# Near keys per 64 queries, two heads side by side in the partitions, and one near score bank at a time

## The chip, the cores and the metric

The kernel runs on one NeuronCore of a Trainium2 chip. The metric is the device time of one execution in microseconds. Nothing is shared with other cores; the input is the same in every run.

## The reference, cut to what matters

A layernorm over `x` (4 x 2048 x 256, f32) feeds two branches that are added to `x`: a linear layer on values rounded to fp8, and an attention with 16 heads of width 16. In the attention, query `i` sees key `j` only if `j` is a multiple of 4 ("far" keys, 512 of them, the same for every query) or if it is close ("near" keys):

```python
allowed = (j % STRIDE == 0) | (jnp.abs(i - j) <= LOCAL)      # STRIDE 4, LOCAL 8
scores = jnp.where(allowed, scores, -jnp.inf)
attn = jax.nn.softmax(scores, axis=-1)
out = jnp.einsum('bhqk,bhkd->bhqd', attn, v)
```

The softmax subtracts the true maximum of each row, so the scores are made twice: once to find each query's maximum and once, with the maximum already subtracted, for the exponential.

## The kernel before

**Two stages.** `part_project` makes q, k, v and the linear branch, 512 rows at a time, and writes q, k and v to DRAM tables. `part_attend` then walks 64 steps: 4 batches x 4 groups of 4 heads (16 iterations) x 4 chunks of 512 queries. Every step's instructions are written out for each engine, so the order of work on TensorE (PE) is the order of calls in `tensor_attend`'s `body`.

**The heads of a group** are numbered h = 2p + f: f picks the half of the array's rows in which q and k of the head lie (partitions 0-50 or 64-114; `half(f)`), p is the pair. q and k are each three fp16 parts (48 rows), and 3 more rows carry the negated maximum.

**What a step does on each engine:**

- PE, maxima: 8 calls `far_unit(tile, p)` (L1105): queries of one 128-row tile against 512 far keys for both f, into two PSUM banks (`ps_u`, two such pairs of banks). 2 calls `near_unit(tiles)` (L1110 to L1127): for each of two query tiles, a mask matmul (L1116, 216 columns) and then 2 x 2 matmuls of 108 columns (L1123): the near window of 128 queries has 108 keys that are no multiples of 4.
- DVE: one `tensor_reduce` for each unit (L1012 far, 1024 elements; L1015 near, 864 elements), then `maximum()` (L995); POOL splits the result in bf16 parts (`negmax`), PE transposes it (`maxima`, L1061), ACT copies it (L946), and SP moves it into the q operand of the next step (L859). The maxima run ahead of the scores: the first AHEAD units of a step's list belong to the next step, the others to the one after.
- PE, scores: 8 calls `far(r, p)` (L1070): 128 far keys x 512 queries for both f, one PSUM bank each. 2 calls `near(p)` (L1072 to L1086): for each of 4 query tiles, two mask matmuls (L1080) and two score matmuls (L1083), 128 columns each, for both f at once, into two banks of 108 partitions.
- The banks of the scores are a ring of three (`S_BANKS`, `ps_s`): before it writes a bank, PE waits in `free_score` until ACT has read what was in it three entries before. A step has 21 entries: 16 far, 4 near, 1 for the maxima.
- ACT: one `Exp` for each score bank (L953 far, L958 near), 512 columns each, one copy of the result (L937, `copy_out`, after the bank of far (1,3)), one small copy of the maxima.
- PE, weighing (f32): `weigh(r)`: for each of 4 far rounds, 4 heads in 4 column strips of the array, 512 columns (L1142); for the near keys, 4 tiles x 4 heads, 128 columns (L1149). An f32 matmul appears as two instructions. All go into bank `ps_o`: one group of three rounds belongs to the step before, two to the step itself.
- SP issues all DMAs in one order: q and k of steps ahead (L90, L92, L100), v of the iteration ahead (`load_v`, one DMA for the far and three for the near keys, in four pieces over two steps), the sums (L851), shares and results.

**PE's order in a step of before** (W is a `weigh`, `u` a far unit, `nu` a near unit):

```
u(2,1) far(0,0) | W2 | far(0,1) u(1,0) u(0,0) far(2,1) | W3 | far(1,0) nu(0) u(2,0) far(1,1) | W4 near keys |
near(0) u(3,1) u(1,1) far(2,0) | W0 | maxima far(3,1) u(3,0) nu(1) far(3,0) | W1 | near(1) u(0,1)
```

Of the kernel before, what the change touches and what calls it, by code (L numbers as in the profile page):

```python
# [45 lines left out]
HALF = P // 2  # L46
# [4 lines left out]
MASK_K = WPAD + S - NS + WPAD  # L51
# [7 lines left out]
VR = D + 1  # L59
EPS = 1e-5  # L60
BANDS = ((1, 18), (6, 6), (21, 5))
# [17 lines left out]
def half(f, n=KR):  # L79

    return slice(f * HALF, f * HALF + n)
# [21 lines left out]
def part_project(nc, io, dram, keep, ctx):  # L103

    with ExitStack() as memory:
# [31 lines left out]
        v_sb = sb("v_sb", [P, 2, TT, NH, VR])  # L137
# [72 lines left out]
        def sync_project(sp):  # L210
# [13 lines left out]
            sp.dma_start(keep["mask_k"][:], io["near_k"].bitcast(BF16)).then_inc(keep["bands_loaded"], 16)  # L224
            sp.dma_start(keep["mask_q"][:], io["near_q"].bitcast(BF16)).then_inc(keep["bands_loaded"], 16)
# [53 lines left out]
        def gpsimd_project(pool):  # L279
# [5 lines left out]
            nc.gpsimd.memset(v_sb[:, 0, :, :, D:VR], 1.0).then_inc(v_set, 1)  # L285
            nc.gpsimd.memset(v_sb[:, 1, :, :, D:VR], 1.0).then_inc(v_set, 1)
# [23 lines left out]
        def scalar_project(act):  # L310
# [6 lines left out]
            def body(j, n):  # L317
# [27 lines left out]
                if main:  # L345
# [7 lines left out]
                    if not (isinstance(c, int) and c < 2):  # L353
                        act.wait_ge(v_stored[k], 16 * earlier(j, n))
                    nc.scalar.activation(
                        v_sb[:, k].rearrange("p t h w -> p (t h) w")[:, :, 0:D],
                        ps_v.rearrange("p a (t w) -> p (a t) w", w=D), ACT.Copy).then_inc(v_copied, 1)
# [267 lines left out]
UNITS = TT * PAIRS + TT // 2  # L625
# [3 lines left out]
AHEAD = 5  # L629
# [5 lines left out]
    ("near", 0), ("far", 2, 0), ("negmax",), ("far", 3, 1), ("far", 3, 0),  # L635
    ("near", 1),
# [3 lines left out]
    ("far", 2, 1), ("far", 1, 0), ("far", 0, 0), ("near", 0), ("far", 2, 0),  # L640
    ("far", 3, 1), ("far", 1, 1), ("far", 3, 0), ("near", 1), ("far", 0, 1),
# [17 lines left out]
def part_attend(nc, io, dram, keep, out, ctx, done):  # L659
# [69 lines left out]
    k_op, mask_k, mask_q = keep["k_op"], keep["mask_k"], keep["mask_q"]  # L729
    v_op = [keep["v_op"], sb("v_op1", [P, NS // P + S // P, HG * VR])]  # L730
    probs = sb("probs", [P, ROUNDS, HG, CH])
# [53 lines left out]
    def window(p, tile):  # L785
        return p * S + WSTEP * tile
# [3 lines left out]

    def close(tile):
        return WSTEP * tile
# [39 lines left out]
    def sync_attend(sp):  # L832
        def load_v(it, par, windows=range(-1, STRIDE - 1)):

            v = dram["v"][it // G, :, it % G * HG * VR:(it % G + 1) * HG * VR]
            for r in windows:
                if r < 0:
                    to, src = v_op[par][:, 0:NS // P, :], v[LOCAL:LOCAL + S, :].rearrange(
                        "(c p r) w -> r p c w", p=P, r=STRIDE)[0]
                else:  # L840
                    to = v_op[par][r:WIN:STRIDE - 1, NS // P:, :]
                    src = bass.AP(tensor=v.tensor, offset=v.offset + (1 + r) * NH * VR,
                                  ap=[[STRIDE * NH * VR, WIN // 3], [P * NH * VR, S // P], [1, HG * VR]])
                sp.dma_start(to, src).then_inc(v_loaded[par], 16)
# [69 lines left out]
        for k in range(2):  # L914
            sp.wait_ge(done["qk_stored"][k], 16 * 12 * B * CPB // 2)
            sp.wait_ge(done["v_stored"][k], 16 * B * CPB // 2)
        load_v(0, 0)
# [11 lines left out]
    def scalar_attend(act):  # L929
# [9 lines left out]
        def body(st):  # L939
            todo = st.entries()  # L940
            for kind in todo:
# [12 lines left out]
                else:  # L954
                    h = kind[1]
# [23 lines left out]
    def vector_attend(dve):  # L979

        def body(st):
# [16 lines left out]
            for i, kind in enumerate(MAXIMA):  # L998
# [14 lines left out]
                else:  # L1013
                    tile = 2 * kind[1]
                    ins = nc.vector.tensor_reduce(peak_near[:, :, tile:tile + 2].rearrange("q f t p -> q f (t p)"),  # L1015
                                                  banks[:, :, 0:2 * PAIRS * WIN].rearrange("q f (g w) -> q f g w",
# [344 lines left out]
```

## Time and profile before

| what | value |
| --- | --- |
| median of 3 runs | 1126.22 us (1123.71 to 1129.16) |
| span of the profiled execution | 1127.2 us; no time of its own is listed for that execution |
| busy: PE, DVE, ACT, POOL | 95%, 84%, 72%, 22% |
| attention steps | from about 247 us to about 1055 us of the span |
| projection, final projection | before and behind them |

A page of the profile lists busy time by engine, the span in 40 slices, the chain that ended last, and groups of instructions (line, engine, operation, output and inputs with shapes, count; then busy time and mean duration, and the idle time before them with what ended it). PEld is the weight load of a matmul, a separate instruction. The busy time of PE counts a matmul from its start to its modelled end, so back-to-back short matmuls overlap in it.

### The profile page before, as it was taken

The numbers are of one execution on the slowest core, as the hardware profiler recorded it, in microseconds if no ns is written. First come the engines' busy times: TensorE is split into PE (matmuls) and PEld (weight loads), VectorE is DVE, ScalarE is ACT, GpSimd is POOL, SyncE is SP. The second block draws the span as 40 slices with busy tenths as digits, with TensorE's granted clock in tenths as the row PEclk, the third lists the DMA queues.
The fourth block names the chain that finished last, engine by engine and source line by source line (L and its number), as shares of the span: only waits on it lengthen the run. The fifth ranks groups of instructions, "written<-read, shape, count | busy, mean of one in ns | idle before, by whom it ended". The sixth has DMA issues, their size and how long they took to land.

```text
span 1127.2 us, 28640 instructions
## 1 busy us (share of the span) xinstructions
PE 1070.1 (95%) x10945; PEld 484.3 (43%) x10945; DVE 948.4 (84%) x1203; ACT 811.9 (72%) x1524; POOL 248.4 (22%) x381
## 2 busy tenths in 40 slices
PE   5899999969999999999999999999999999999898
PEld 3566666623333333333333333333333333333387
DVE  5888877588999999999999999999898999999133
ACT  2444344327988898888888888888898888888700
POOL 1433333301121212212121212212121212222100
PEclk9999999968999999999999999999999999999999
DMA  6566666641232333333332333333333333231167
GB/s 188 184 197 206 206 209 209 196 111 44 81 87 81 99 91 85 87 103 104 95 107 82 112 91 105 89 96 111 94 99 93 99 94 94 86 84 48 55 216 246
DMA packets 167066, 134.21 MB, mean 119 GB/s; under 512 B 70652, under 2 KB 146172, under 8 KB 166924
## 3 DMA queue, kind: packets, MB, share of 16 engines
q1 hardware_dynamic: 164344, 128.19, 38.4%
q10 hardware_dynamic: 2592, 4.26, 1.1%
q8 instruction: 85, 1.39, 0.5%
q14 instruction: 45, 0.37, 0.1%
HBM read 71.26 MB, written 59.84 MB: 116 GB/s over the span
## 4 chain that ended last, share of the span: by engine, by line
PE 74%; DVE 12%; issue 7%; DMA 5%; ACT 2%; SPq 0%; DVEq 0%; ACTq 0%
PE ps_attend L1142 15%; PE ps_attend L1070 11%; DVE peak_far L1012 10%; PE ps_attend L1105 9%; PE ps_attend L1149 5%; PE ps_attend L1222 5%; PE ps_project L607 5%; PE ps_project L597 5%; PE ps_project L576 4%; PE ps_attend L1080 4%; DMA sums<-out_rows 3%; PE ps_attend L1116 3%; PE ps_project L540 2%; PE ps_attend L1083 2%; PE ps_attend L1123 2%
## 5 line engine op out<-in xcount | busy, mean ns | idle before, releaser
L1012 DVE TENSOR_REDUCE peak_far<-ps_attend 128x2 f32<-128x1024 f32 x512 | 608.7, 1221 | 42.7 <-PE ps_attend L1105 31.3
L953 ACT ACTIVATE probs<-ps_attend 128x512 f32<-128x512 f32 x1024 | 541.4, 598 | 49.4 <-PE ps_attend L1070 46.2
L1142 PE MATMUL ps_attend<-probs,v_op 128*17 128x512 f32 x2048 | 270.2, 600 | 0.0
L1070 PE MATMUL ps_attend<-q_op,k_op 51*128 51x512 f16 x1024 | 254.2, 387 | 4.9 <-ACT probs L953 3.3
L1105 PE MATMUL ps_attend<-k_op,q_op 48*128 48x512 f16 x1024 | 187.9, 388 | 25.7 <-DVE peak_far L1012 15.3
L958 ACT ACTIVATE probs<-ps_attend 108x512 f32<-108x512 f32 x256 | 138.9, 594 | 35.7 <-PE ps_attend L1083 35.7
L1070 PEld LDWEIGHTS ps_attend<-q_op,k_op 51*128 51x128 f16 x1024 | 76.8, 93 | 195.6 <-ACT probs L953 137.4
L819 POOL CAST negmax<-peak 128x16 bf16<-128x16 f32 x64 | 12.7, 198 | 612.8 <-DVE peak L995 612.8
L1015 DVE TENSOR_REDUCE peak_near<-ps_attend 128x8 f32<-128x864 f32 x128 | 131.0, 1023 | 10.5 <-PE ps_attend L1123 10.4
L810 POOL TENSOR_TENSOR out_rows<-out_rows,share_rows 128x512 f32<-128x512 f32 x64 | 81.4, 1272 | 65.4 <-DMA share_rows<-shares_dram 63.0
L1105 PEld LDWEIGHTS ps_attend<-k_op,q_op 48*128 48x128 f16 x1024 | 49.7, 94 | 98.6 <-DVE peak_far L1012 71.6
L1080 PEld LDWEIGHTS ps_attend<-mask_q,mask_k 48*108 48x108 bf16 x1024 | 60.0, 125 | 69.4 <-ACT probs L953 56.1
L1080 PE MATMUL ps_attend<-mask_q,mask_k 48*108 48x128 bf16 x1024 | 78.7, 228 | 0.8 <-ACT probs L953 0.8
L1083 PE MATMUL ps_attend<-q_op,k_op 51*108 51x128 f16 x1024 | 73.6, 218 | 0.0
L1149 PE MATMUL ps_attend<-probs,v_op 108*17 108x128 f32 x2048 | 68.3, 274 | 0.0
L328 ACT ACTIVATE qk_parts<-ps_project,ranges 128x1024 f16<-128x1024 f32 x16 | 17.8, 1114 | 68.6 <-PE ps_project L576 62.0
L297 POOL TENSOR_TENSOR quant<-quant,power 128x1024 f32<-128x1024 f32 x16 | 37.7, 2357 | 116.9 <-DVE qk_parts L436 80.3
L1116 PE MATMUL ps_attend<-mask_k,mask_q 48*128 48x216 bf16 x512 | 59.0, 260 | 4.1 <-DVE peak_far L1012 1.6
L1083 PEld LDWEIGHTS ps_attend<-q_op,k_op 51*108 51x108 f16 x1024 | 61.5, 126 | 0.0
L576 PE MATMUL ps_project<-xnT,wq 128*128 128x512 f32 x128 | 60.2, 614 | 1.2 <-ACT xnT L335 1.2
L1142 PEld LDWEIGHTS ps_attend<-probs,v_op 128*17 128x17 f32 x2048 | 34.0, 95 | 59.3 <-issue 58.6
L1123 PE MATMUL ps_attend<-k_op,q_op 48*128 48x108 f16 x1024 | 58.4, 210 | 0.0
(82 smaller groups left out, 1037.9 us busy)
## 6 DMA issues: line engine op xcount, KB each, us to landing
share_rows<-shares_dram SPq DMA_DIRECT2D x64, 256.0 KB
attn_dram<-out_rows SPq DMA_DIRECT2D x64, 256.0 KB, 5.5
q_dram<-qk_parts SPq DMA_DIRECT2D x96, 128.0 KB
k_dram<-qk_parts SPq DMA_DIRECT2D x96, 128.0 KB
q_op<-q_dram SPq DMA_DIRECT2D x128, 96.0 KB, 2.4
k_op<-k_dram SPq DMA_DIRECT2D x64, 144.0 KB, 3.1
v_dram<-v_sb SPq DMA_DIRECT2D x16, 544.0 KB, 5.1
base<-in_x SPq DMA_DIRECT2D x16, 512.0 KB, 5.2
```

The costliest lines, as they stand in the source:

```text
L576: last = nc.tensor.matmul(ps_q[:, m], wq[:, i, m * P:(m + 1) * P], xnT[:, k, i], start=(i == 0), stop=(i == KC - 1))
L953: ins = nc.scalar.activation(probs[:, r, h], ps_s[st.bank(kind)], ACT.Exp, scale=undo)
L958: ins = nc.scalar.activation(probs[0:WIN, ROUNDS - 1, h], ps_s[st.bank(kind)][0:WIN], ACT.Exp, scale=undo)
L1012: ins = nc.vector.tensor_reduce(peak_far[:, :, p, tile], banks, AX_X, ALU.max)
L1015: ins = nc.vector.tensor_reduce(peak_near[:, :, tile:tile + 2].rearrange("q f t p -> q f (t p)"), banks[:, :, 0:2 * PAIRS * WIN].rearrange ...
L1070: nc.tensor.matmul(bank, k[half(f, KM), keys], q[half(f, KM), p], start=True, stop=True).then_inc(s_ready, 1)
L1080: nc.tensor.matmul(banks[f][0:WIN, cols], mask_k[half(f), at_mask:at_mask + WIN], mask_q[half(f), tile * P:(tile + 1) * P], start=True, st ...
L1083: ins = nc.tensor.matmul(banks[f][0:WIN, cols], k[half(f, KM), at:at + WIN], q[half(f, KM), p, cols], start=False, stop=True)
L1105: nc.tensor.matmul(banks[f], q[half(f), p, tile * P:(tile + 1) * P], k[half(f), strided(p):strided(p) + NS], start=True, stop=True).then_i ...
L1116: nc.tensor.matmul(banks[f][:, whole].rearrange("q (p w) -> q p w", p=PAIRS), mask_q[half(f), st.queries(d) * CH + tile * P:st.queries(d) ...
L1142: ins = nc.tensor.matmul(ps_o[h * VW:h * VW + VR], v[:, r, h * VR:(h + 1) * VR], probs[:, r, h], start=(r == 0), stop=False)
L1149: ins = nc.tensor.matmul(ps_o[h * VW:h * VW + VR, t * P:(t + 1) * P], v[0:WIN, tile, h * VR:(h + 1) * VR], probs[0:WIN, r, h, t * P:(t + 1 ...
```

## The change

**Window.** A window of near keys now belongs to 64 queries (`HALF`), not 128: 60 keys (`WIN`), 32 windows per row of 2048.

**Near scores.** `near()` fills two banks, one for each p. Bank p holds head f = 0 in partitions 0-59 and head f = 1 in 64-123. For each bank by itself: wait for it, one mask matmul of 512 columns (62 rows, 124 output partitions), then 8 tiles x 2 f score matmuls of 64 columns (51 rows, 60 outputs: half of the rows and half of the columns of the array), and one semaphore increment. A step has 19 ring entries instead of 21, and ACT makes 2 near exponentials of 124 x 512 instead of 4 of 108 x 512. `probs_near` has two buffers.

**Near maxima.** One near unit a step: two mask matmuls of 480 columns (one for each f) and 4 x 2 x 2 x 2 = 32 matmuls of 60 columns (48 rows, 64 outputs: the queries of half a tile). DVE reduces 960 elements once instead of 864 twice. `AHEAD` is 3 instead of 5.

**Weighing.** Near: 8 tiles x 2 pairs, 64 columns, 124 rows and 49 outputs: the v operand (`v_near`) holds zeros where the other head's keys are. v is laid out with the heads of the two pairs interleaved, so weights are read with a step of two; the far round 0 takes 32 outputs instead of 17.

**Loads.** v of an iteration comes in 7 DMAs instead of 4 (near rows of 34 elements for each f); POOL zeroes `v_near` at the start; one mask table instead of two.

**Order.** PE's order in a step becomes:

```
u(2,1) far(0,0) | W2 | u(1,0) far(0,1) u(0,0) far(2,1) | W3 | nu far(1,0) u(2,0) far(1,1) | W4 near keys |
u(3,1) maxima near u(1,1) far(2,0) | W0 | u(3,0) far(3,1) u(0,1) far(3,0) | W1
```

```diff
-WIN = (P + 2 * LOCAL) // STRIDE * (STRIDE - 1)
-WSTEP = P // STRIDE * (STRIDE - 1)
+WIN = (HALF + 2 * LOCAL) // STRIDE * (STRIDE - 1)
+WSTEP = HALF // STRIDE * (STRIDE - 1)
+NEAR = HALF + WIN
+MASK_ROWS = WIN + 2
+VP = 2 * VR
+VT = 2 * VW + VP
+VM = VW + VR
...
+            for par in range(2):
+                nc.gpsimd.memset(keep["v_near"][par][:], 0.0).then_inc(pads_set, 1)
...
-UNITS = TT * PAIRS + TT // 2
+UNITS = TT * PAIRS + 1
-AHEAD = 5
+AHEAD = 3
...
+                for f in range(2):
+                    to = v_near[par][f * HALF + r:f * HALF + WIN:STRIDE - 1, :, f * 2 * VW:f * 2 * VW + VP]
+                    src = bass.AP(tensor=v.tensor, offset=v.offset + (1 + r) * NH * VR + f * VP,
+                                  ap=[[STRIDE * NH * VR, WIN // 3], [HALF * NH * VR, NT], [1, VP]])
+                    sp.dma_start(to, src).then_inc(v_loaded[par], 16)
...
-                    if kind in OPENS and st.n >= 1:
-                        act.wait_ge(pv_done, ROUNDS * st.at())
-                    ins = nc.scalar.activation(probs[0:WIN, ROUNDS - 1, h], ps_s[st.bank(kind)][0:WIN], ACT.Exp,
-                                               scale=undo)
+                    if kind in OPENS and st.n >= 2:
+                        act.wait_ge(pv_done, ROUNDS * st.at(-1))
+                    ins = nc.scalar.activation(probs_near[0:NEAR, st.n % 2, kind[1]], ps_s[st.bank(kind)][0:NEAR],
+                                               ACT.Exp, scale=undo)
...
+        def score_near(st):
 
             q, k = q_op[:, st.slot()], k_op[st.parity()]
+            for p in range(PAIRS):
+                bank = free_score(st, ("near", p))
+                nc.tensor.matmul(bank[0:NEAR], masks[half(p, MASK_ROWS), MASK_KS],
+                                 masks[half(p, MASK_ROWS), shown(MASK_Q, HALF, st.queries())], start=True, stop=False)
+                for t in range(CH // HALF):
+                    cols, at = slice(t * HALF, (t + 1) * HALF), window(p, st.queries() * CH // HALF + t)
+                    for f in range(2):
+                        ins = nc.tensor.matmul(bank[half(f, WIN), cols], k[half(f, KM), at],
+                                               q[half(f, KM), p, cols], start=False, stop=(t == CH // HALF - 1))
+                ins.then_inc(s_ready, 1)
...
+            for f in range(2):
+                mask = masks[half(f, MASK_ROWS), shown(MASK_K, WIN, st.queries(d))]
+                nc.tensor.matmul(banks[f][:, 0:TT * PAIRS * WIN].rearrange("q (t p w) -> q t p w", t=TT, p=PAIRS),
...
+            for t in range(TT):
                 for p in range(PAIRS):
...
+                    for u in range(2):
+                        tile = 2 * t + u
+                        at = window(p, st.queries(d) * CH // HALF + tile)
+                        for f in range(2):
+                            ins = nc.tensor.matmul(
+                                banks[f][half(u, HALF), (t * PAIRS + p) * WIN:(t * PAIRS + p + 1) * WIN],
+                                q[half(f), p, tile * HALF:(tile + 1) * HALF], k[half(f), at],
...
+                n = VW if r == 0 else VR
                 for h in range(HG):
+                    ins = nc.tensor.matmul(ps_o[h * VW:h * VW + n], far[:, columns_of(r, h, n)], probs[:, r, h],
                                            start=(r == 0), stop=False)
             else:
                 pe.wait_ge(s_used, st.entry(LASTS["near",], d))
+                for t in range(CH // HALF):
+                    tile, cols = st.queries(d) * CH // HALF + t, slice(t * HALF, (t + 1) * HALF)
+                    for p in range(PAIRS):
+                        ins = nc.tensor.matmul(ps_o[half(p, VM), cols], near[0:NEAR, tile, p:p + 2 * VM - 1:2],
+                                               probs_near[0:NEAR, (st.n + d) % 2, p, cols],
+                                               start=False, stop=(t == CH // HALF - 1))
```

## Rows read from the trace of the kernel before

**Rows 1.** The page: busy time of PE, granted clock in 40 slices.

```profile
PE 1070.1 (95%) x10945; PEld 484.3 (43%) x10945; DVE 948.4 (84%) x1203; ACT 811.9 (72%) x1524; POOL 248.4 (22%) x381
...
PEclk9999999968999999999999999999999999999999
```

**Rows 2.** Groups from 400 to 1000 us, shapes apart: busy, mean ns, idle before.

```profile
L1012 DVE TENSOR_REDUCE peak_far<-ps_attend 128x2 f32<-128x1024 f32 x377 | 448.3, 1221 | 27.4 <-PE ps_attend L1105 18.6 <-issue 1.1
L953 ACT ACTIVATE probs<-ps_attend 128x512 f32<-128x512 f32 x754 | 398.7, 597 | 36.7 <-PE ps_attend L1070 34.4
L1142 PE MATMUL ps_attend<-probs,v_op 128*17 128x512 f32 x1504 | 197.9, 598 | 0.0
...
L958 ACT ACTIVATE probs<-ps_attend 108x512 f32<-108x512 f32 x188 | 102.0, 594 | 25.6 <-PE ps_attend L1083 25.6
L1015 DVE TENSOR_REDUCE peak_near<-ps_attend 128x8 f32<-128x864 f32 x94 | 96.0, 1022 | 7.9 <-PE ps_attend L1123 7.9
```

**Rows 3.** Timeline of PE, one step of 12.62 us: start, length, line, count.

```profile
602.38 0.23 PE L1061 MATMUL ps_attend<-ident_bf,negmax 128*128 128x128 bf16 x1
602.55 0.39 PE L1070 MATMUL ps_attend<-q_op,k_op 51*128 51x512 f16 x2
602.77 0.38 PE L1105 MATMUL ps_attend<-k_op,q_op 48*128 48x512 f16 x2
603.20 0.27 PE L1116 MATMUL ps_attend<-mask_k,mask_q 48*128 48x216 bf16 x2
603.30 0.26 PE L1123 MATMUL ps_attend<-k_op,q_op 48*128 48x108 f16 x4
603.39 0.26 PE L1116 MATMUL ps_attend<-mask_k,mask_q 48*128 48x216 bf16 x2
...
603.94 1.05 PE L1142 MATMUL ps_attend<-probs,v_op 128*17 128x512 f32 x8
604.92 0.26 PE L1080 MATMUL ps_attend<-mask_q,mask_k 48*108 48x128 bf16 x2
605.02 0.22 PE L1083 MATMUL ps_attend<-q_op,k_op 51*108 51x128 f16 x2
605.08 0.22 PE L1080 MATMUL ps_attend<-mask_q,mask_k 48*108 48x128 bf16 x2
...
606.59 1.05 PE L1142 MATMUL ps_attend<-probs,v_op 128*17 128x512 f32 x8
607.58 0.39 PE L1070 MATMUL ps_attend<-q_op,k_op 51*128 51x512 f16 x2
...
608.97 1.05 PE L1142 MATMUL ps_attend<-probs,v_op 128*17 128x512 f32 x8
609.96 0.39 PE L1070 MATMUL ps_attend<-q_op,k_op 51*128 51x512 f16 x2
...
611.35 1.07 PE L1149 MATMUL ps_attend<-probs,v_op 108*17 108x128 f32 x32
612.35 0.26 PE L1080 MATMUL ps_attend<-mask_q,mask_k 48*108 48x128 bf16 x2
...
612.86 0.64 PE L1105 MATMUL ps_attend<-k_op,q_op 48*128 48x512 f16 x4
...
614.02 1.05 PE L1142 MATMUL ps_attend<-probs,v_op 128*17 128x512 f32 x8
615.00 0.23 PE L1061 MATMUL ps_attend<-ident_bf,negmax 128*128 128x128 bf16 x1
```

**Rows 4.** Timeline of PE's weight loads in that step: in brackets the wait before.

```profile
611.03 0.09 PEld L1070 LDWEIGHTS ps_attend<-q_op,k_op 51*128 51x128 f16 x1 [0.18 <-ACT probs L953]
```

**Rows 5.** Timeline of ACT in that step.

```profile
610.38 2.08 ACT L953 ACTIVATE probs<-ps_attend 128x512 f32<-128x512 f32 x4 [0.29 <-PE ps_attend L1070]
...
613.05 1.08 ACT L958 ACTIVATE probs<-ps_attend 108x512 f32<-108x512 f32 x2
```

**Rows 6.** Timeline of the DMA issues on SP, the same step.

```profile
615.57 1.61 SPq L859 DMA_DIRECT2D q_op<-negmax_rows  x2
```

More of the change, by code:

```diff
@@ L634 @@
     ("far", 0, 0), ("far", 0, 1), ("far", 2, 1), ("far", 1, 0), ("far", 1, 1),
-    ("near", 0), ("far", 2, 0), ("negmax",), ("far", 3, 1), ("far", 3, 0),
-    ("near", 1),
+    ("negmax",), ("near", 0), ("far", 2, 0), ("far", 3, 1), ("far", 3, 0),
 )
@@ L639 @@
 MAXIMA = (
-    ("far", 2, 1), ("far", 1, 0), ("far", 0, 0), ("near", 0), ("far", 2, 0),
-    ("far", 3, 1), ("far", 1, 1), ("far", 3, 0), ("near", 1), ("far", 0, 1),
+    ("far", 2, 1), ("far", 1, 0), ("far", 0, 0), ("near",), ("far", 2, 0),
+    ("far", 3, 1), ("far", 1, 1), ("far", 3, 0), ("far", 0, 1),
 )
@@ L785, in window, with columns_of, shown @@
     def window(p, tile):
-        return p * S + WSTEP * tile
+        at = p * S + WSTEP * tile
+        return slice(at, at + WIN)
+    def columns_of(r, h, n):
+        first = (r * 2 + h % 2) * VP + h // 2
+        return slice(first, first + 2 * n - 1, 2)
+    def shown(columns, tile, queries):
+        first = columns.start + (0 if queries == 0 else 2 if queries == CPB - 1 else 1) * tile
+        return slice(first, first + columns.stop - columns.start - 2 * tile)
     def strided(p):
         return WPAD + p * S + S - NS
-    def close(tile):
-        return WSTEP * tile
     def gpsimd_attend(pool):
@@ L1129, in weigh @@
-        def weigh(st, d, r, tiles=range(TT)):
-            v = v_op[st.parity(d)]
+            for f in range(2):
+                mask = masks[half(f, MASK_ROWS), shown(MASK_K, WIN, st.queries(d))]
+                nc.tensor.matmul(banks[f][:, 0:TT * PAIRS * WIN].rearrange("q (t p w) -> q t p w", t=TT, p=PAIRS),
+                                 masks[half(f, MASK_ROWS), MASK_QS],
+                                 mask.rearrange("r (t w) -> r t w", t=TT).unsqueeze(2).broadcast_to(
+                                     [MASK_ROWS, TT, PAIRS, WIN]), start=True, stop=False)
@@ L1132, in weigh @@
+        def weigh(st, d, r):
+            far, near = v_far[st.parity(d)], v_near[st.parity(d)]
             if r == 0:
                 if st.queries(d) == 0:
-                    pe.wait_ge(v_loaded[st.parity(d)], 64 * (st.half_iteration(d) + 1))
+                    pe.wait_ge(v_loaded[st.parity(d)], 16 * 7 * (st.half_iteration(d) + 1))
                 if st.n + d >= 1:
@@ L1158, in far_unit, with near_unit @@
                 unit(st, ("far", tile, p))
-            def near_unit(tiles):
-                unit(st, ("near", tiles))
+            def near_unit():
+                unit(st, ("near",))
             def far(r, p):
@@ L1173, in maxima, with weigh_last @@
                     score_peaks(st)
-            def weigh_last(r, tiles=range(TT)):
+            def weigh_last(r):
                 if st.exists(-1):
-                    weigh(st, -1, r, tiles)
+                    weigh(st, -1, r)
             def weigh_own(r):
@@ L1195, in body @@
             weigh_last(4)
-            near(0)
             far_unit(3, 1)
+            maxima()
+            near()
             far_unit(1, 1)
```

145 lines of the change are left out of this document (54 added, 91 removed).

## The prediction

> **What bounds the kernel now.** I read the page first: PE is busy 95% of the span at full granted clock over nearly all slices [rows 1]. That number alone misleads, because a short matmul counts until its modelled end. So I then read the groups of the attention stage, and last the timeline of one step on each engine. The near reduction L1015 ran 94 times in 600 us, so 47 steps took 12.77 us each on average [rows 2]; most repeat one pattern of 12.62 us (602.38 to 615.00) [rows 3], and a few take some tenths longer. DVE has 8 far reductions at about 1.17 us apart and 2 near ones: it is busy for some 11.8 us of the 12.62. ACT's 21 reads of PSUM take less: four exponentials need 2.08 us [rows 5], about 0.5 each. Neither fills the step, and PE's own streams don't either.
>
> What sets the step is seen in PE's timeline when it is cut at the five weighs. A far weigh takes 0.98 us (606.59 to 607.58), the near one 1.00 (611.35 to 612.35) [rows 3]. Between them lie five gaps, each of which fills four score banks. With three banks in the ring, the fourth fill must wait for the exponential of the first. For the gap before W4: far(1,0) starts at 609.96, its exponential at 610.38 [rows 5], it lasts 0.60, the freed bank's weight load starts at 611.03 after a wait on ACT [rows 4], 512 columns at 2.4 GHz are 0.21, and the weigh starts at 611.35, which leaves 0.11 for emptying the array before its f32 column strips begin. So a gap that opens with a far pair costs 1.40 (607.58 to 608.97, 609.96 to 611.35, 602.55 to 603.94), one that opens with near(p) costs 1.67 (612.35 to 614.02, 604.92 to 606.59) [rows 3]. The sum is 3 x 1.40 + 2 x 1.67 + 0.16 for the maxima + 4 x 0.98 + 1.00 = 12.62. That is the measured step: **a chain of PE streams and one exponential's latency per gap**, in which units hide for nothing between the first and the fourth fill.
>
> **The change, gap by gap.** DVE saves about 2 x 1.02 - 1.13 = 0.9 us a step (864 elements take 1.02, 1024 take 1.22, so 960 take about 1.13) and ACT two exponentials, 1.0 us [rows 2, 5]. In this account both are worth nothing: the cover is the PE chain, and each keeps more than 1.5 us of slack. What counts is what PE does between the weighs.
>
> A pair of 512-column matmuls costs a slot of 0.22 (602.55 to 602.77) [rows 3]. In the new order one unit stands before the first far pair of three gaps, where no exponential hides it.
> - Before W3 and before W1: 0.22 + 1.40 = 1.62 each, 3.24 together.
> - Before W2, one unit and one far pair, the ring not full: 0.22 + 0.22 + 0.11 for emptying = 0.55.
> - Before W4: nu + 1.40.
> - Before W0: u(3,1) 0.22, emptying 0.11 because the maxima matmul uses the whole array, maxima 0.16, near bank 0 (N), near bank 1 (N), u(1,1) and far(2,0). The second bank of far(2,0) reuses near bank 0. From that bank's end to the weigh is 1.16 at least (near(0) of before ends at 612.86, W0 starts at 614.02 [rows 3]), or else N + 0.22 + 0.22 + 0.11, whichever is longer.
>
> *N.* The mask is 512 columns, 0.22. The 16 fills go in 8 pairs (f = 0 and 1 in opposite corners of the array). In before, two matmuls of different row halves start together (a group x2 is as long as one) and a pair takes 0.06 at 128 columns (605.02 to 605.08); a pair of 108 columns takes about 0.048 (x4 from 603.30 to 603.39) [rows 3]. At 64 columns a pair lies between 0.027 (the columns alone) and 0.059 (the nearest row); I take 0.035, nearer the columns, since both rows scale with them, so 0.28. Mask and fills use different shapes of the array. Where before changes shape it pays about 0.11: the maxima matmul holds PE 0.17 (602.38 to 602.55) for 128 columns, which are 0.05 [rows 3]. No row shows this particular change, from 64 x 128 to 64 x 64; bounds 0 and 0.11. I take 0.11, since every change of shape that rows show pays it, and twice per bank (in and out). N = 0.22 + 0.28 + 0.22 = 0.72.
>
> *nu.* The mask: 216 columns take 0.10 (603.20 to 603.30) [rows 3], 480 take 0.21. The 32 fills use all four corners; the far weigh shows four column strips at once (8 matmuls of 0.60 in 1.05) [rows 2, 3], so I take 8 groups of four at 0.035, 0.28 (bounds 0.22, and 32 x 0.030 = 0.96 if they go one by one at half the pair rate of before). Two changes of shape, 0.22. nu = 0.71, against 0.38 for each of two before (two halves of 0.19, 603.20 to 603.39) [rows 3].
>
> *Near weigh.* 32 matmuls of 64 columns, two strips at once, stream exactly as much as 32 of 128 columns, four at once. The weights are 49 columns instead of 17; hidden as long as a load is shorter than its stream. 1.00 to 1.44 (if two such loads go one after the other: 49 f32 columns in two passes are 0.041 each at 2.4 GHz, against a stream of 0.053 for both); I take 1.05. Round 0 with 32 outputs: nothing to 0.03, hidden in a stream of 0.43.
>
> The gap before W0 is 0.22 + 0.11 + 0.16 + 0.72 + max(1.16, 0.72 + 0.55) = 2.48. The step: 3.24 + 0.55 + (0.71 + 1.40) + 2.48 + 3.92 + 1.05 = **13.35 us against 12.62: +0.73, times 64 steps = +47 us**. Against the profiled execution (span 1127.2, no other time listed for it) that is 1174; the three runs have a median of 1126.2, 1 us below its span, so the forecast is **1173 us**.
>
> The rest is hidden, and its price if the cover goes is small: the POOL zeroing ends long before POOL's first sum; the first scores come one near reduction earlier, at most 1 us gained [rows 2]; three more v DMAs per iteration sit on SP ahead of the sums, shares and maxima. The maxima's DMA is the one to watch: it was issued from 615.57 to 617.18 [rows 6], 4.8 us after W4's end, and far(0,0) needs it. In the new order far(0,0) comes 2.37 + 0.98 + 1.62 + 0.98 + 0.22 = 6.2 us after W4's end; in before it was 1.67 + 0.98 + 0.16 + 1.40 + 0.98 + near(1) 0.51 (as 612.35 to 612.86) + two units 0.44, also about 6.2 [rows 3]. So nothing is taken. If it were late by a whole 1 us in half of the steps, that is 32 us. Behind the waiting far(0,0) all of PE would stand.
>
> A rule of the Trainium skill speaks against the change. TensorEngine Tiling, Key Properties, says that changing the tiling mode drains TensorE; in its terms, mask and fill are different modes. The rows agree for the changes that before makes (0.11 each); without any such cost at the fills the forecast would be the rival "no emptying" below.
>
> **The rivals.**
> 1. *No emptying between mask and fills*, everything else as forecast: N = 0.50, nu = 0.49, gap before W0 0.49 + 0.50 + 1.16 = 2.15, step 12.80; +0.18, +12 us: 1138 (1130 to 1146). For it: only the column half changes, and the row halves stay. Against: entering and leaving the maxima matmul costs.
> 2. *The small matmuls go one at a time.* Near fills alone: N = 0.22 + 16 x 0.030 + 0.22 = 0.92, gap 2.88, step +1.13, +72 us: 1199. The unit's as well: nu = 1.39, step +1.81, +116 us: 1242. For it: the fills of f = 0 and 1 now write one bank, where in before they wrote two; and there are twice as many small matmuls for the columns. Against: in before pairs start together. The Trainium skill bears on it: TensorEngine Tiling, Gotcha 1, says that different row tiles can't access the same PSUM bank simultaneously, which would give the first of these two times; TensorE: Matmul & The Clock Gate, Part 1, puts the least distance of two matmul starts at about 25 ns, which would give nearly the second. No row shows one bank written by both halves; against the second rule, rows show starts together in different tiles.
> 3. *Faster: masks and fills stream side by side.* A mask occupies one row half only; if the fills of the other half run beside it and no shape change costs anything, N = 0.43, nu = 0.42, the gap before W2 0.44, the gap before W0 0.38 + 0.43 + 1.16 = 1.97, the near weigh 0.95; step 3.24 + 0.44 + 1.82 + 1.97 + 3.92 + 0.95 = 12.34, -0.28, -18 us: 1108. It decides as soon as near stage, near unit and near weigh together fall under the 2.78 us that they take in before. For it: DVE and ACT are then lighter, so nothing else holds the step. Against: the 0.11 at every change of shape.
>
> **Chances and range.** Forecast 0.48 (own range 1148 to 1192), rival 1 0.13, rival 2 0.19, rival 3 0.16, late DMAs or something unseen 0.04. The range reaches down to rival 3's neighbourhood and up between the two forms of rival 2: 1112 to 1225. A measurement tells about 0.5%, 5.6 us, from no change: faster 0.16; within 0.5% a part of rivals 1 and 3, 0.10; slower 0.74.
>
> **What would show it.** Right: a step of about 13.3 us; three gaps of about 1.6 (one 2.1) where the fourth fill waits for ACT; PE starting the first fill 0.3 after its mask and the pairs of fills 0.03 to 0.04 apart; DVE and ACT with clearly more idle time ended by PE. Wrong: fills 0.015 or less apart per matmul with no pause behind the mask (rivals 1, 3), or 0.025 to 0.03 per matmul (rival 2); a weight load of far(0,0) that waits for a DMA; a near weigh well over 1.1 us. The weakest number is the pause at a change of shape: six of them a step, 42 us in all.

## The result

The changed kernel takes **1160.53 us** (median of 4 runs, 1159.62 to 1161.34) against 1126.45 (4 runs) before: ratio **1.0307**, 95% interval 1.0286 to 1.0328, so 34 us or 3.1% slower. The forecast was 1173, +47 us, by a step of 13.35 us instead of 12.62.

The page of the changed kernel: PE is busy as before, DVE and ACT have lost the work that the change takes from them (49 and 64 us of busy time, against [rows 1]), and the time went up.

```profile
PE 1082.1 (93%) x11713; PEld 468.0 (40%) x11713; DVE 899.3 (78%) x1139; ACT 747.5 (64%) x1396; POOL 253.8 (22%) x383
...
PEclk9999999959999999999999999999999999999999
```

The groups of the changed kernel from 400 to 1000 us (busy, mean ns, idle before it), which answer to [rows 2]: 46 near reductions in 600 us, so about 13.0 us a step by this count, and DVE and ACT idle far longer in front of far work, both ended by PE.

```profile
L1030 DVE TENSOR_REDUCE peak_far<-ps_attend 128x2 f32<-128x1024 f32 x362 | 435.7, 1215 | 78.9 <-PE ps_attend L1120 77.0
L972 ACT ACTIVATE probs<-ps_attend 128x512 f32<-128x512 f32 x724 | 378.5, 600 | 109.4 <-PE ps_attend L1087 109.4
...
L1032 DVE TENSOR_REDUCE peak_near<-ps_attend 128x16 f32<-128x960 f32 x46 | 53.3, 1158 | 20.2 <-PE ps_attend L1137 19.3 <-PE ps_attend L1120 0.8
```

PE's timeline over one step of the changed kernel (start, length, line, shapes, count), which answers to [rows 3]. L1165 is the near weigh, L1158 the far one, L1120 a far unit, L1087 far scores, L1094 and L1099 mask and fills of a near bank, L1127 and L1137 those of the near unit.

```profile
602.65 1.10 PE L1165 MATMUL ps_attend<-probs_near,v_near 124*49 124x64 f32 x32
603.69 0.39 PE L1120 MATMUL ps_attend<-k_op,q_op 48*128 48x512 f16 x2
604.01 0.23 PE L1078 MATMUL ps_attend<-ident_bf,negmax 128*128 128x128 bf16 x1
604.17 0.42 PE L1094 MATMUL ps_attend<-masks 62*124 62x512 bf16 x1
604.52 0.42 PE L1099 MATMUL ps_attend<-q_op,k_op 51*60 51x64 f16 x16
604.88 0.42 PE L1094 MATMUL ps_attend<-masks 62*124 62x512 bf16 x1
605.24 0.42 PE L1099 MATMUL ps_attend<-q_op,k_op 51*60 51x64 f16 x16
...
606.13 1.07 PE L1158 MATMUL ps_attend<-probs,v_far 128*32 128x512 f32 x8
607.13 0.39 PE L1120 MATMUL ps_attend<-k_op,q_op 48*128 48x512 f16 x2
...
608.42 0.39 PE L1087 MATMUL ps_attend<-q_op,k_op 51*128 51x512 f16 x1 [0.25 <-ACT probs L972]
608.74 1.05 PE L1158 MATMUL ps_attend<-probs,v_far 128*17 128x512 f32 x8
609.73 0.39 PE L1120 MATMUL ps_attend<-k_op,q_op 48*128 48x512 f16 x2
...
610.26 1.05 PE L1158 MATMUL ps_attend<-probs,v_far 128*17 128x512 f32 x8
611.25 0.39 PE L1120 MATMUL ps_attend<-k_op,q_op 48*128 48x512 f16 x2
...
612.86 1.05 PE L1158 MATMUL ps_attend<-probs,v_far 128*17 128x512 f32 x8
613.85 0.38 PE L1127 MATMUL ps_attend<-masks 62*128 62x480 bf16 x2
614.15 0.44 PE L1137 MATMUL ps_attend<-k_op,q_op 48*64 48x60 f16 x32
614.53 0.39 PE L1087 MATMUL ps_attend<-q_op,k_op 51*128 51x512 f16 x2
...
615.92 1.11 PE L1165 MATMUL ps_attend<-probs_near,v_near 124*49 124x64 f32 x32
```

Cut at the weighs, it reads term by term against the prediction:

| term | forecast | measured | from |
| --- | --- | --- | --- |
| near weigh | 1.05 | 1.04 | 602.65 to 603.69 |
| gap before W0 | 2.48 | 2.44 | 603.69 to 606.13 |
| a near bank, N | 0.72 | 0.71 | 604.17 to 604.88 |
| gaps before W1 and W3 | 1.62 each | 1.61 each | 607.13 to 608.74, 611.25 to 612.86 |
| gap before W2 | 0.55 | 0.53 | 609.73 to 610.26 |
| near unit | 0.71 | 0.68 | 613.85 to 614.53 |
| gap before W4 | 2.11 | 2.07 | 613.85 to 615.92 |
| four far weighs | 3.92 | 3.97 | 1.00 + 3 x 0.99 |
| step | 13.35 | 13.27 | 602.65 to 615.92 |

Every term lies within 0.05 us. A fourth fill still waits for ACT in the gaps before W1, W3 and W4 (the wait of 0.25 at 608.42 is one of them). Yet 64 x 0.65 is 42 us, and 34 were measured. Between the fourth and the last copy of the maxima (L946, L965) lie 60 steps: 764.1 us in before, 12.735 each, and 795.9 in the changed kernel, 13.264 each. Nearly all steps of the changed kernel are alike; before had some that took up to 13.8. The difference of these sums is 31.8 us, that of the two spans 32.3. The spans also tell of which executions the traces are: each run of the changed kernel takes 1.8 us more than its span (1161.34 against 1159.5), so the profiled execution of before, of 1127.2, would take about 1129.0 (an estimate), 2.6 above the median. Its irregular steps are then probably more than those of a median execution.

DVE waits for the DMA of the sums in some of these steps (engine, line, waited for: total, times, longest, 400 to 1000 us of before); the changed kernel's waits have no such row.

```profile
DVE shares L988 <- DMA sums<-out_rows: 7.4, 8, 1.4
```

### The profile page after: what moved, and what is told of

Same layout as the page of the kernel before. It is cut to its first block, busy times and chain, and to the rows that moved or that the text cites. A ratio compares the mean times of both kernels' runs of the same rounds, so it can differ in the third digit from the quotient of the medians.

```text
span 1159.5 us, 29841 instructions
## 1 busy us (share of the span) xinstructions
PE 1082.1 (93%) x11713; PEld 468.0 (40%) x11713; DVE 899.3 (78%) x1139; ACT 747.5 (64%) x1396; POOL 253.8 (22%) x383
## 4 chain that ended last, share of the span: by engine, by line
PE 84%; ACT 10%; DVE 2%; DMA 2%; issue 1%; SPq 0%; DVEq 0%; ACTq 0%
PE ps_attend L1158 22%; PE ps_attend L1087 14%; ACT probs L972 10%; PE ps_attend L1120 9%; PE ps_attend L1165 6%; PE ps_attend L1234 4%; PE ps_project L615 4%; PE ps_project L605 4%; PE ps_project L584 4%; PE ps_attend L1094 4%; PE ps_attend L1099 4%; PE ps_project L548 2%; PE ps_attend L1137 2%; PE ps_attend L1127 2%; PE ps_project L594 1%
## 5 line engine op out<-in xcount | busy, mean ns | idle before, releaser
L1087 PE MATMUL ps_attend<-q_op,k_op 51*128 51x512 f16 x1024 | 271.5, 384 | 49.0 <-ACT probs L972 48.8
L1158 PE MATMUL ps_attend<-probs,v_far 128*17 128x512 f32 (+1 forms) x2048 | 272.2, 604 | 0.0
L1120 PE MATMUL ps_attend<-k_op,q_op 48*128 48x512 f16 x1024 | 201.6, 389 | 8.1 <-DVE peak_far L1030 6.1
L1087 PEld LDWEIGHTS ps_attend<-q_op,k_op 51*128 51x128 f16 x1024 | 69.7, 95 | 171.3 <-ACT probs L972 149.5
L1120 PEld LDWEIGHTS ps_attend<-k_op,q_op 48*128 48x128 f16 x1024 | 49.4, 93 | 201.0 <-issue 103.4
L976 ACT ACTIVATE probs_near<-ps_attend 124x512 f32<-124x512 f32 x128 | 76.4, 597 | 35.5 <-PE ps_attend L1099 28.2
L1032 DVE TENSOR_REDUCE peak_near<-ps_attend 128x16 f32<-128x960 f32 x64 | 74.1, 1158 | 28.7 <-PE ps_attend L1137 27.7
L1165 PE MATMUL ps_attend<-probs_near,v_near 124*49 124x64 f32 x2048 | 70.7, 222 | 0.0
L1158 PEld LDWEIGHTS ps_attend<-probs,v_far 128*17 128x17 f32 (+1 forms) x2048 | 36.2, 100 | 81.2 <-issue 56.6
L1165 PEld LDWEIGHTS ps_attend<-probs_near,v_near 124*49 124x49 f32 x2048 | 61.3, 125 | 15.1 <-issue 15.1
L615 PE MATMUL ps_project<-wv,xnT 128*128 128x256 f32 x256 | 57.9, 379 | 0.0
L605 PE MATMUL ps_project<-xnT,wk 128*128 128x512 f32 x128 | 57.6, 593 | 0.0
L1094 PE MATMUL ps_attend<-masks 62*124 62x512 bf16 x128 | 54.9, 429 | 0.0
L1099 PE MATMUL ps_attend<-q_op,k_op 51*60 51x64 f16 x2048 | 54.8, 194 | 0.0
L615 PEld LDWEIGHTS ps_project<-wv,xnT 128*128 128x128 f32 x256 | 48.6, 190 | 13.4 <-issue 7.7
```

The source lines that it names most:

```text
L605: last = nc.tensor.matmul(ps_k[:, m], wk[:, i, m * P:(m + 1) * P], xnT[:, k, i], start=(i == 0), stop=(i == KC - 1))
L615: last = nc.tensor.matmul(ps_v[:, t // 2, t % 2 * H:(t % 2 + 1) * H], xnT[:, k, i, t * P:(t + 1) * P], wv[:, i], start=(i == 0), stop=(i = ...
L1087: nc.tensor.matmul(bank, k[half(f, KM), keys], q[half(f, KM), p], start=True, stop=True).then_inc(s_ready, 1)
L1094: nc.tensor.matmul(bank[0:NEAR], masks[half(p, MASK_ROWS), MASK_KS], masks[half(p, MASK_ROWS), shown(MASK_Q, HALF, st.queries())], start=T ...
L1099: ins = nc.tensor.matmul(bank[half(f, WIN), cols], k[half(f, KM), at], q[half(f, KM), p, cols], start=False, stop=(t == CH // HALF - 1))
L1120: nc.tensor.matmul(banks[f], q[half(f), p, tile * P:(tile + 1) * P], k[half(f), strided(p):strided(p) + NS], start=True, stop=True).then_i ...
```

## The experiments

Each ran in turn with the kernel before on one chip, so the ratios to before are the numbers to compare; times in parentheses are ratio x 1126.45. For the changed kernel the ratio is 1.0307.

### Masks in the shape of the fills

```diff
-                nc.tensor.matmul(bank[0:NEAR], masks[half(p, MASK_ROWS), MASK_KS],
-                                 masks[half(p, MASK_ROWS), shown(MASK_Q, HALF, st.queries())], start=True, stop=False)
+                for f in range(2):
+                    n, at = (HALF, WIN)[f], MASK_KS.start + f * HALF
+                    nc.tensor.matmul(bank[half(f, n)], masks[half(f, MASK_ROWS), at:at + n],
+                                     masks[half(f, MASK_ROWS), shown(MASK_Q, HALF, st.queries())],
+                                     start=True, stop=False)
```

> The changed kernel with each near bank's mask made by two matmuls on the two opposite corners of the array that the fills use (64 rows x 64 columns each, 512 columns, both side by side) instead of one matmul on 64 x 128. Shape-change theory: the two pauses inside each bank go, so a bank takes about 0.22 + 0.25 instead of 0.71 us, the gap before W0 falls from 2.44 to about 2.1 (near bank 0's end plus 1.16 becomes its floor), the step by 0.3, the time by about 20 us from 1160.5 to 1140. Rival, the extra time of a near bank is the price of many small matmuls: there are now two more of them, so no gain, 1160 to 1162.

Ratio 1.0151, 1.0131 to 1.0170 (1143.5): 17 us gained. PE's timeline of this kernel, from the near weigh's end to W0:

```profile
607.27 0.39 PE L1123 MATMUL ps_attend<-k_op,q_op 48*128 48x512 f16 x2
607.60 0.23 PE L1078 MATMUL ps_attend<-ident_bf,negmax 128*128 128x128 bf16 x1
607.75 0.40 PE L1096 MATMUL ps_attend<-masks 62*64 62x512 bf16 x2
608.00 0.40 PE L1102 MATMUL ps_attend<-q_op,k_op 51*60 51x64 f16 x16
608.24 0.38 PE L1096 MATMUL ps_attend<-masks 62*64 62x512 bf16 x2
608.46 0.40 PE L1102 MATMUL ps_attend<-q_op,k_op 51*60 51x64 f16 x16
...
609.41 1.07 PE L1161 MATMUL ps_attend<-probs,v_far 128*32 128x512 f32 x8
```

The same 16 fills take 0.24 (608.00 to 608.24) where they took 0.36, and a mask 0.22 to 0.25 where it took 0.35; the bank is 0.49 instead of 0.71 although it has one matmul more. The gap is 2.14, and near bank 0's end to W0 is 1.17, the floor that the prediction had put at 1.16; both banks together are 0.38 shorter (1.04 from 607.75 to 608.79, against 1.42), and this floor keeps 0.08 of it. So the pause of about 0.12 between 64 x 128 and 64 x 64 is real. The mask is still bf16, and the f16 fills still add to it, so neither of these makes the pause. The small matmuls cost little more than their columns, 0.030 for a pair.

### Both near banks masked, then both filled

```diff
-            for p in range(PAIRS):
-                bank = free_score(st, ("near", p))
+            banks = [free_score(st, ("near", p)) for p in range(PAIRS)]
+            for p, bank in enumerate(banks):
                 nc.tensor.matmul(bank[0:NEAR], masks[half(p, MASK_ROWS), MASK_KS],
                                  masks[half(p, MASK_ROWS), shown(MASK_Q, HALF, st.queries())], start=True, stop=False)
+            for p, bank in enumerate(banks):
                 for t in range(CH // HALF):
```

> The changed kernel with both near banks claimed and masked first and then both filled, instead of bank by bank. Shape-change theory: two of the four changes of shape at the near banks go; the gap before W0 falls by 0.2 us, the time by about 12 us to 1148. Rival, claiming both banks at once waits for ACT longer than it saves: no gain or a loss of up to 10 us. Rival, pauses don't depend on shape: no change.

Ratio 1.0221, 1.0199 to 1.0243 (1151.3): 9 to 10 us gained over the changed kernel. Its typical step is 13.10 instead of 13.27, 64 x 0.17 = 11 us. Claiming the second bank early cost nothing. The number was met, but not for the reason expected:

```profile
612.66 0.39 PE L1121 MATMUL ps_attend<-k_op,q_op 48*128 48x512 f16 x2
...
613.14 0.43 PE L1094 MATMUL ps_attend<-masks 62*124 62x512 bf16 x2
613.50 0.67 PE L1100 MATMUL ps_attend<-q_op,k_op 51*60 51x64 f16 x32
...
614.94 1.07 PE L1159 MATMUL ps_attend<-probs,v_far 128*32 128x512 f32 x8
```

Two of the four changes of shape are gone, and the two masks, which lie in different row halves, now run side by side: 0.36 for both, where one had taken 0.35. The two near banks take 0.96 (613.14 to 614.10) instead of 1.42. Of these 0.46 only 0.16 reach the step. Near bank 0 is filled no sooner: its last fill starts 1.08 behind the near weigh (613.74), against 1.07 in the changed kernel. The last fill of far(2,0) waits for this bank, its weight load stands 0.41 us for ACT, and W0 comes 1.20 after that last near fill, as in the run above. In the changed kernel it came 1.37 after. So the gain is the way down to the floor, not two pauses of 0.11.

### Three units put back under the exponential

```diff
-            far_unit(1, 0)
             far(0, 1)
+            far_unit(1, 0)
...
-            near_unit()
             far(1, 0)
+            near_unit()
...
-            far_unit(3, 0)
             far(3, 1)
+            far_unit(3, 0)
```

> The changed kernel with three neighbours swapped in PE's order: far(0,1) before u(1,0), far(1,0) before the near unit, far(3,1) before u(3,0), so that each gap opens with a far pair and the unit lies under the exponential's latency. Chain theory: two gaps fall from 1.61 to 1.40, one from 2.07 to about 1.45; the step by 1.0 us, the time by 55 to 67 us to about 1100, below the kernel before. Rival, PE's streams are the bound and their order does not matter: no change, 1160. Rival, DVE then gets its units in clumps and becomes the bound: a gain of less than 30 us.

Ratio 0.9837, 0.9817 to 0.9856 (1108.1): 52 us faster than the changed kernel and 18 us faster than before. PE's timeline, the gaps before W4 and W1:

```profile
602.67 0.39 PE L1087 MATMUL ps_attend<-q_op,k_op 51*128 51x512 f16 x2
...
604.10 1.10 PE L1165 MATMUL ps_attend<-probs_near,v_near 124*49 124x64 f32 x32
...
608.58 0.39 PE L1087 MATMUL ps_attend<-q_op,k_op 51*128 51x512 f16 x2
...
609.97 1.05 PE L1158 MATMUL ps_attend<-probs,v_far 128*17 128x512 f32 x8
```

The gaps are 1.43 (expected 1.45) and 1.39 (1.40); the step of 12.20 is 1.07 shorter. 64 x 1.07 would be 68 us. Most of the missing 16 is in irregular steps: the mean of the 60 is 12.424, which makes 60 x 0.22 = 13 us. far(0,0) stood for the DMA of the maxima, up to 2.1 us at a time (columns as above, 400 to 1000 us). PEld and PE are two instruction streams of one engine that stand in the same steps, so the two rows below must not be added.

```profile
PEld ps_attend L1087 <- DMA q_op<-negmax_rows: 13.6, 14, 2.1
...
PE ps_attend L1087 <- DMA q_op<-negmax_rows: 9.4, 9, 1.8
```

### The same three swaps in the kernel before, the other way round

```diff
-            far(0, 1)
             far_unit(1, 0)
+            far(0, 1)
...
-            far(1, 0)
             near_unit(0)
+            far(1, 0)
...
-            far(3, 1)
             far_unit(3, 0)
+            far(3, 1)
```

> The kernel before with nothing but three neighbours of PE's order swapped the way the change has them: u(1,0) ahead of far(0,1), the near unit ahead of far(1,0), u(3,0) ahead of far(3,1). Chain theory: two gaps grow by 0.22 us, one by 0.38, the step from 12.62 to 13.4; with before's scattered DMA waits then covered the time rises by 44 to 52 us to 1170 to 1178, more than the whole change costs. Rival, the change's cost comes from its small matmuls and masks and the order is neutral: no change from before.

Ratio 1.0404, 1.0386 to 1.0421 (1172.0): the order alone costs the kernel before 46 us, more than the whole change costs it. Its typical step is 13.43, as expected (13.4). In PE's timeline the gap before W4 is 1.77 (603.15 to 604.92), where it was 1.40 [rows 3]; the gap before W3 is 1.60 (613.99 to 615.59), and the one before W1 is 1.77 with the maxima's 0.16 in it (608.57 to 610.34):

```profile
603.15 0.27 PE L1116 MATMUL ps_attend<-mask_k,mask_q 48*128 48x216 bf16 x2
...
604.92 1.07 PE L1149 MATMUL ps_attend<-probs,v_op 108*17 108x128 f32 x32
```

### More work for DVE, more work for ACT

The first edit makes the near reduction twice, once into a spare tile that nothing reads:

```diff
+                    nc.vector.tensor_reduce(keep['peak_spare'][:].rearrange("q f t p -> q f (t p)"),
+                                                  banks[:, :, 0:TT * PAIRS * WIN].rearrange("q f (g w) -> q f g w",
+                                                                                            w=WIN), AX_X, ALU.max)
```

> The changed kernel with the near reduction on DVE made a second time into a spare tile, 1.1 us more DVE work per step (69 us in all), more than the change had saved there. Chain theory: DVE has over 2 us of slack per step, so 0 to +6 us. Rival, DVE's work counts in the step: up to +69 us.

Ratio 1.0373, 1.0343 to 1.0402 (1168.5): 7 to 8 us for 69 us of work. The typical step went from 13.27 to 13.35: in the trace u(3,1) starts 1.11 us after the near weigh instead of 1.04 (606.57 to 607.68), since its pair of banks is released later. The expectation of at most 6 us was slightly passed.

```profile
606.57 1.11 PE L1168 MATMUL ps_attend<-probs_near,v_near 124*49 124x64 f32 x32
607.68 0.39 PE L1123 MATMUL ps_attend<-k_op,q_op 48*128 48x512 f16 x2
```

The second adds two exponentials to a step:

```diff
                 ins.then_inc(s_used, 1)
+                if kind in (("far", 2, 3), ("far", 3, 1)):
+                    nc.scalar.activation(keep["spare"][:], keep["wo"][:].rearrange("p k f -> p (k f)"), ACT.Exp)
```

> The changed kernel with two extra exponentials of 128 x 512 on ACT in each step (from SBUF into a spare tile, behind far (2,3) and far (3,1), where ACT stood idle for 1.0 and 0.5 us): 1.1 us more ACT work a step, 70 us in all, about what the change saved there. Chain theory: they lie in idle time and no exponential of a gap starts later, 0 to +5 us. Rival, ACT's work counts in the step: up to +70 us.

Ratio 1.0293, 1.0276 to 1.0310 (1159.5), the interval overlaps that of the changed kernel: nothing for some 70 us of ACT work. ACT's timeline has the extra exponential (L980) in what was idle time:

```profile
606.22 2.07 ACT L972 ACTIVATE probs<-ps_attend 128x512 f32<-128x512 f32 x4 [0.45 <-PE ps_attend L1090]
608.15 0.65 ACT L980 ACTIVATE spare<-wo 128x512 bf16<-128x512 f32 x1
```

So giving ACT back as much as the change took from it, 1.0 us a step, costs nothing where it is idle, and giving DVE back a little more than the 0.9 that it had lost costs 7 to 8 us: so the lighter DVE bought no more than about that. That an exponential in another place of ACT's order would be free as well is not shown.

### Do two halves of the rows write one bank at a time?

```diff
-                for t in range(CH // HALF):
-                    cols, at = slice(t * HALF, (t + 1) * HALF), window(p, st.queries() * CH // HALF + t)
-                    for f in range(2):
+                for f in range(2):
+                    for t in range(CH // HALF):
+                        cols, at = slice(t * HALF, (t + 1) * HALF), window(p, st.queries() * CH // HALF + t)
```

> The changed kernel with the near fills of a bank in another order: all eight tiles of head f = 0, then all eight of f = 1, so that neighbours lie in the same corner of the array and can't run side by side. If fills of opposite corners do overlap in one bank (about 0.03 us per pair in the changed kernel's trace), a bank takes 0.25 us longer, the gap before W0 0.5, the time 30 us more: 1190. Rival, matmuls of two row halves can't write one bank at the same time, so they already go one by one: no change, 1160.

Ratio 1.0473, 1.0450 to 1.0495 (1179.7): 19 us more than the changed kernel, not 30 and not 0. A bank's fills take 0.50 (611.95 to 612.45) instead of 0.36:

```profile
611.95 0.57 PE L1099 MATMUL ps_attend<-q_op,k_op 51*60 51x64 f16 x16
612.45 0.42 PE L1094 MATMUL ps_attend<-masks 62*124 62x512 bf16 x1
```

The rival is refuted: fills of opposite corners do run side by side in one bank. The size was mis-expected, since this order doesn't keep them apart. Read in slices of 0.01 us, the trace has four fills start one after the other up to 612.07, eight more from 612.10 to 612.22, about two every 0.03 us, and then the last four one by one, 0.03 us apart. It doesn't say which fill is which, but this fits f = 1 setting in while f = 0 still has about four to go.

### The scattered waits of before

```diff
-TURN = 8
+TURN = 9
```

> The kernel before with the reciprocal of the sums one reduction later in DVE's order (in front of the last unit of a step instead of the last but one). In before, 8 of 47 steps had DVE wait for the sums' DMA, 7.4 us in 600, and the mean step was 12.77 instead of 12.62; in the changed kernel that wait is gone. If this wait is what makes before's steps irregular, and so what the change gave back beside its longer steps: a gain of 5 to 9 us on before, ratio 0.992 to 0.996. Rival, the irregular steps come from something else: ratio 1.000 or above.

Ratio 0.9983, 0.9970 to 0.9996: 2 us, not 5 to 9. DVE's wait for the sums is gone from this kernel's waits, but far(0,0) now waits for the maxima's DMA, which it never did in before (300 to 1000 us, columns as above):

```profile
PEld ps_attend L1070 <- DMA q_op<-negmax_rows: 6.7, 26, 0.9
```

Its mean step is 12.647 instead of 12.735 in its one profile, 5.3 us in 60 steps, of which the two spans keep 3.3 (1127.2 and 1123.9). That before's profile is of an execution slower than its median is part of the rest. So the wait for the sums is part of before's irregular steps, and behind it stands the next DMA, almost as late. Four steps of 12.90 to 12.92, one in 16, are in both traces; their cause is open. The changed kernel has the reciprocal of the sums in front of its last unit too, for its `TURN` is 8 of nine units. But a longer step alone takes most of the wait away: in the run above with before's units first, a step of 13.43, DVE waited 2.1 us for the sums from 300 to 1000 us, against 7.4 in before.

### The maxima's DMA ahead of the second piece, and all together

Both kernels below have this edit on SP, and the three swaps:

```diff
                 move_sums(st)
-            load_piece(st, 1)
             if ("negmax",) in st.entries():
                 move_negmax(st)
+            load_piece(st, 1)
```

> The swapped order of the earlier run (three units hidden) with one more edit: SP issues the DMA of the maxima ahead of the second piece of k or v instead of behind it. In that run's trace far(0,0) waited 23 us of 600 for this DMA, in steps whose v pieces stood ahead of it. DMA theory: these waits go, worth 15 to 30 us: 1080 to 1095 against 1108. Rival, the wait moves to k, v or the sums: less than 5 us gained.

Ratio 0.9731, 0.9713 to 0.9749 (1096.1): 12 us under the run with the swaps alone; expected were 15 to 30. The mean step is 12.207 (it was 12.424), its typical one 12.20, so the waits are gone and there was no more to gain from them. The expectation was too high because its 23 us are the two rows above added, 13.6 and 9.4, which are largely the same waits seen twice.

Where the DMA had been late is seen in SP's queue in the run with the swaps alone. The two near DMAs of v ahead of the maxima's two transfers take 1.7 us to issue. But in nine steps the issue of the two itself took 2.3 to 3.7 us instead of 1.5 to 1.6, and these nine are those behind the nine fetches of finished heads (L782, two DMAs of 256 KB):

```profile
622.31 1.34 SPq L782 DMA_DIRECT2D heads<-attn_dram  x2
...
631.00 1.67 SPq L862 DMA_DIRECT2D v_near<-v_dram  x2
632.72 2.94 SPq L877 DMA_DIRECT2D q_op<-negmax_rows  x2
...
644.46 1.66 SPq L862 DMA_DIRECT2D v_near<-v_dram  x2
646.16 1.54 SPq L877 DMA_DIRECT2D q_op<-negmax_rows  x2
```

In the 21 other steps with the same two v DMAs ahead it took 1.54 to 1.55, once 1.87, so these v DMAs alone don't stretch it. With the maxima's DMA ahead of them it takes 1.52 to 1.61 in every step. How the fetch comes to act a step later is open.

The last one adds the corner masks of the first experiment, the same for the near unit (four mask matmuls of 64 outputs), and the maxima matmul right behind W4:

```diff
-            far_unit(3, 1)
             maxima()
+            far_unit(3, 1)
```

> Everything that the account says is loss taken out of the changed kernel: masks on the corners for near banks and near unit, three units hidden, the maxima matmul right behind W4, the maxima's DMA ahead of the second piece. Account: gaps 1.39 + 1.39 + 1.39 + 0.53 + 2.04, weighs 5.01, step 11.75 us; times 64 that is 29 us under the swapped order's 12.20, so about 1060 to 1070 if the maxima's DMA is in time. Rival, DVE (10.9 us of work a step, two pairs of banks) becomes the bound: 12.0 to 12.2 us a step, 1080 to 1095.

Ratio **0.9566**, 0.9548 to 0.9585 (1077.6): 4.3% faster than before, 83 us faster than the changed kernel, but 8 us over the expected range. PE's timeline of its step, 11.89 us long:

```profile
603.78 0.23 PE L1078 MATMUL ps_attend<-ident_bf,negmax 128*128 128x128 bf16 x1
603.94 0.39 PE L1123 MATMUL ps_attend<-k_op,q_op 48*128 48x512 f16 x2
604.26 0.40 PE L1096 MATMUL ps_attend<-masks 62*64 62x512 bf16 x2
...
605.91 1.07 PE L1163 MATMUL ps_attend<-probs,v_far 128*32 128x512 f32 x8
```

The gap before W0 is 2.13, as with the corner masks alone: with the maxima first, the pause moved from before them to behind the unit (603.94 to 604.26 is 0.32 for a slot of 0.22). The near unit gained nothing either: its pause between mask and fills became one between the far pair ahead of it and the mask. The account had counted both as gains, 0.14 us a step, 9 us. The mean step is 11.989, 0.1 over the typical one; the trace shows waits for the sums and for the maxima's DMA again. The rival, DVE as the bound, lay at 12.0 to 12.2 us a step; the typical step of 11.89 still has PE's gaps of 1.39 and 1.44, and PE stood for DVE only 2.5 us in 600, so DVE is not the bound yet. But it idles only about 1.1 us of such a step (0.61, 0.22 and 0.23), so little room is left below it.

## Why the prediction was right, and where it was off

**The bound.** Right. PE's chain with one exponential's latency per gap gave 12.62 for before and every gap of the changed kernel within 0.05 us. The swaps in both directions (52 us gained, 46 lost) and 70 us of extra work on ACT for nothing show it. "DVE and ACT worth nothing" holds for ACT; for DVE it holds but for 7 to 8 us, the price of its near reduction made twice.

**Units in front of the first far pair.** Right: 1.61, 1.61 and the near unit in full. This is what made the kernel slower. With these swaps undone, the same change is faster than before. The prediction summed this loss but did not single it out; it called the pauses the weakest number. Those are the smaller part: taking three of the four at the near banks away gave 17 us.

**The pause at a change of shape.** Taken as 0.11 from other shapes, bounds 0 and 0.11; the corner masks show 0.10 to 0.13 per change. The two changes of one near bank cost 0.22 of its 0.71 us. The rule of the Trainium skill (TensorEngine Tiling, Key Properties: changing the tiling mode drains TensorE) agrees with these runs.

**The small matmuls.** Taken as 0.035 per pair, measured 0.030; with the pause a little over 0.11 the two small errors nearly cancel in N (0.71 for 0.72), which is luck. The unit's 32 fills take 0.38 with the pause behind them, so four at a time, as taken. Rival 2 is refuted, also in the form of the Trainium skill's TensorEngine Tiling, Gotcha 1: with outputs in different partitions of one bank the two row halves did overlap, a pair every 0.030 us. Rival 1 and rival 3 are refuted by the pauses.

**The near weigh.** 1.04, taken as 1.05.

**The size.** The forecast of +47 us was 13 us above the measured 34. Two terms of the sum were mis-sized. The step was put at 13.35 and is 13.27: 5 us. And the sum compared it with before's typical step of 12.62, while before's mean is 12.735: 60 x 0.115 = 7 us of irregular steps, of which the changed kernel has next to none. The prediction had seen the mean of 12.77 in the groups and did not carry it into the sum; that these steps would even out in the longer one was in no term. The wait for the sums' DMA is the larger part of them (5.3 of the 7 us, by the trace of the run that moves it), the four steps of 12.90 are another 1.1 us, and their cause is open. That 5 and 7 nearly make 13 is in part luck: before's trace is of an execution some 2.6 us over its median, the changed kernel's 0.8 over its own, and outside the 60 steps the changed kernel costs 0.5 us, where four more steps at +0.65 would be 2.6. These two nearly cancel.

**The maxima's DMA.** Rightly named as the one to watch and rightly costed at nothing: the changed kernel waited for it 0.5 us in 600. The working has a slip, 2.37 for the gap that it sums to 2.48 elsewhere; far(0,0) came 6.26 us after W4's end (603.69 to 609.95), and 6.2 was written. It became the next wait as soon as the step fell to 12.20.

## What to carry to other kernels

When engines wait for each other through a small ring, cut the bounding engine's timeline at the points that recur, and ask for each gap what its length is made of; work that fits between the first fill and the freed bank was free here, and the same work one place earlier cost its full length. Some 70 us of work given back to an engine with slack cost nothing on ACT and 7 to 8 us on DVE, while reordering three calls was worth 52 us. Keep matmuls of one array shape together, and make a mask in the shape of the matmuls that it belongs to; but count the changes along the whole sequence, since removing one may only move it to the next neighbour, and look for the floor behind it: 0.46 us taken from two near banks moved the step by 0.16. A wait of PE and one of its weight loads can be one wait seen twice; what such waits cost is read from the step's mean length.

## What the runs showed of the hardware

- A change of the array's shape cost PE 0.10 to 0.13 us: from 64 x 128 to 64 x 64 (16 fills take 0.36 with it and 0.24 without), from 64 x 128 to the whole array (603.69 to 604.01, 0.32 for a slot of 0.22), and from 64 x 128 to f32 column strips (608.42 to 608.74, 0.32 for 0.21).
- Matmuls of 64 columns in opposite corners of the array run two at a time into the same PSUM bank, 0.030 us per pair; 32 of 60 columns in four corners take at most 0.38, pause included, 0.012 each.
- Two mask matmuls of 512 columns in different row halves, into two banks, ran side by side: 0.36 us for both with the pause, against 0.35 for one.
- Two DMAs of 640 rows of 136 bytes each, ahead in SP's queue, did not by themselves stretch the issue of the next two small DMAs (1.54 to 1.55 us in 20 of 21 steps). In the nine steps that followed a fetch of two times 256 KB it took 2.27 to 3.72 us at a step of 12.20, and 1.55 to 1.97 at the changed kernel's 13.27.
